# Two cross-attention layers on one core: another order in the prologue, one set of row scales for layer two, GpSimd's subtractions later in their window

## The reference

```python
q, k, v = x @ Wq, text @ Wk, text @ Wv
k_ip, v_ip = ip @ Wk_ip, ip @ Wv_ip
# layer one, each head
out = softmax(q k^T / sqrt(32)) v + softmax(q k_ip^T / sqrt(32)) v_ip
# layer two, each head; text_probs is over the full width of 640
text_probs = softmax(q @ k_text^T * scale)
sem = ((text_probs @ text) @ ip^T) * scale
ip_probs = softmax(q k_ip^T * scale + 0.5 * sem) * spatial_mask
out = softmax(q k^T * scale) v + ip_probs v_ip
x = out @ Wo + bo + x
```

## Time and profile before

| | us |
|---|---|
| median of three timed runs | 1839.28 |
| the profiled execution's own time | 1835.73 |
| its span, first to last instruction | 1833.9 |
| PE busy | 1763.1 (96%) |
| DVE busy | 1208.7 (66%) |
| ACT busy | 777.4 (42%) |
| POOL busy | 429.2 (23%) |

### The profile page before, as it was taken

How to read it: one execution, slowest core, us unless ns; L and a number is a source line. 1 busy time by engine, 2 the same in 40 slices (tenths; PEclk the granted TensorE clock), 3 DMA queues, 4 the chain that set the end, 5 groups by cost and what they waited for, 6 DMA issues and landing times. The chain is left out here.

```text
span 1833.9 us, 52042 instructions
## 1 busy us (share of the span) xinstructions
PE 1763.1 (96%) x22067; PEld 1420.8 (77%) x22067; DVE 1208.7 (66%) x2967; ACT 777.4 (42%) x1569; POOL 429.2 (23%) x520
## 2 busy tenths in 40 slices
PE   7988999999999999998999899999999999999998
PEld 4667888888888888885566688888888888888884
DVE  5775676767676767554654376767676767676673
ACT  3243554545545455453222243434444435344351
POOL 3031423334242433321100011211121212122120
PEclk9999999999999999999999999999999999999999
DMA  6742443434334344334146322414142324223221
GB/s 255 159 168 75 137 146 114 148 94 142 107 130 135 109 128 123 114 121 172 58 37 176 109 68 52 124 43 132 51 118 65 105 64 118 58 86 97 79 64 45
DMA packets 123583, 198.36 MB, mean 108 GB/s; under 512 B 41704, under 2 KB 110712, under 8 KB 116760
## 3 DMA queue, kind: packets, MB, share of 16 engines
q1 hardware_dynamic: 117880, 164.50, 31.4%
q10 hardware_dynamic: 5472, 30.54, 4.7%
HBM read 133.91 MB, written 60.88 MB: 106 GB/s over the span
## 5 line engine op out<-in xcount | busy, mean ns | idle before, releaser
L513 PE MATMUL proj<-w_hl,cbuf 128*128 128x128 f16 x9600 | 601.1, 219 | 0.7 <-issue 0.7
L513 PE MATMUL proj<-cbuf,w_hl 128*128 128x322 f16 (+1 forms) x3840 | 591.5, 300 | 2.7 <-issue 2.2
L513 PEld LDWEIGHTS proj<-w_hl,cbuf 128*128 128x128 f16 x9600 | 548.5, 98 | 2.8 <-issue 1.0
L513 PEld LDWEIGHTS proj<-cbuf,w_hl 128*128 128x128 f16 x3840 | 367.4, 97 | 166.5 <-issue 2.8
L1252 POOL TENSOR_TENSOR arena<-arena 128x400 f16<-128x400 f32 x240 | 235.9, 983 | 893.1 <-ACT arena L1011 893.1
L1010 ACT ACTIVATE arena<-st,rs 128x400 f16<-128x400 f32 x480 | 287.2, 598 | 285.3 <-DVE st L1634 167.7
L986 ACT ACTIVATE arena<-proj 128x323 f16<-128x323 f32 (+1 forms) x160 | 70.7, 442 | 516.5 <-PE proj L513 503.3
L1011 ACT ACTIVATE arena<-st,rs 128x400 f32<-128x400 f32 x480 | 285.8, 595 | 0.0
L1553 DVE TENSOR_TENSOR arena<-arena 128x400 f16<-128x400 f32 x240 | 144.9, 604 | 134.8 <-ACT arena L1011 131.7
L662 PE MATMUL pv<-arena 128*128 128x34 f16 (+3 forms) x3840 | 191.9, 189 | 6.9 <-POOL arena L1252 5.7
L662 PEld LDWEIGHTS pv<-arena 128*128 128x128 f16 x3840 | 173.5, 97 | 30.3 <-POOL arena L1252 9.4
(11 more groups left out here) (156 smaller groups left out, 1651.2 us busy)
## 6 DMA issues: line engine op xcount, KB each, us to landing
arena<-k_dram SPq DMA_DIRECT2D x240, 185.2 KB, 3.6
k_dram<-arena SPq DMA_DIRECT2D x160, 161.2 KB, 1.9
c_dram<-cbuf SPq DMA_DIRECT2D x16, 1290.0 KB, 6.4
raw<-ctx_dram SPq DMA_DIRECT2D x14, 1290.0 KB, 7.9
cbuf<-c_dram SPq DMA_DIRECT2D x12, 1290.0 KB
cbuf<-w_dram ACTq DMA_DIRECT2D x24, 640.0 KB, 7.3
arena<-q_dram SPq DMA_DIRECT2D x48, 125.0 KB, 2.6
cbuf<-c_dram ACTq DMA_DIRECT2D x2, 2580.0 KB
```

The costliest lines, as they stand in the source:

```text
L513: mm = nc.tensor.matmul(out, x[a](k), w[b](k), start=(k == 0 and m == 0), stop=(k == KT - 1 and m == 2))
```

## The change

- Start: a semaphore `warm` and 44 small matmuls on PE ahead of the q tiles. The text is loaded in two halves, one on SP's queue ahead of the constants, one on ACT's ahead of the weights (before: whole, on SP, behind the constants). DVE reduces the text first, then waits for the constants; half of the first weight's reductions, `weight_max` and `weight_scale` come behind the text's scale. PE turns the text's maxima ahead of q_tile(0, 1, 0). ACT splits the text ahead of the q tiles' evictions of the second half, and the first weight among them.
- SP at the first units: q and k are stored first and spread after; row 1's context (and its issue, which was ACT's) goes behind unit 1's k. ACT's waits on `kt_out` and `vt_out` go.
- PE: waits on `w_low` before the banks, each bank for itself (`vt`, `odd`); `odd_unit` waits for k's low of bank c only.
- Layer two's scales of all eight rows are made at once in `all_scales` (`rs1`, `back1`), `new_scale` and `row_scales` leave its windows.
- GpSimd in layer one's windows g = 1: `split_context` of slices 1 and 3 both behind the low of tile 5.
- PE in layer two's windows g = 3: three k's instead of two ahead of `max_scores(n, 0)`.

The diff, cut:

```diff
         def _(sp):
-            def place_q(r):
+            def store_q(r):
                 sp.wait_ge(q_lo_ok, r + 1)
                 if r >= 2:
                     sp.wait_ge(qp_in[r % 2], placed(r - 2, 48))
                     sp.wait_ge(s_full, NT * G * (r - 1))
                 sp.dma_start(qd[r % 2], qhl[:, :, 0:G * S]).then_inc(qw_out, 16)
+
+            def spread_q(r):
+
                 sp.wait_ge(qw_out, 16 * (r + 1))
                 for m, part in enumerate((0, 1, 0)):
                     sp.dma_start(qp[m * D:(m + 1) * D, r % 2, 0:G * Q4].rearrange("p (h q) -> p h q", h=HG),
                                  qd[r % 2][:, part].rearrange("(h d) q -> d h q", h=HG)).then_inc(qp_in[r % 2], 16)
-            def place_k(n):
+            def store_k(n):
                 b, g = n // G % B, n % G
                 for part, written in enumerate((k_high, k_low)):
                     sp.wait_ge(written, 2 * n + 2)
                     sp.dma_start(kd[b, g, :, part, IPO:KW], khl[:, part]).then_inc(kw_out[part], 16)
+
+            def spread_k(n):
+
+                b, g = n // G % B, n % G
                 need(sp, s_full, NT * (n - 1))
                 sp.wait_ge(kw_out[0], 16 * (n + 1))
                 for m in range(2):
...
             sp.dma_start(x_first, x_d[0]).then_inc(x_in[0], 16)
+            sp.dma_start(raw[:, 0:TH], text_d[:, 0:TH]).then_inc(text_in[0], 16)
             sp.dma_start(const[:], const_d).then_inc(const_in, 16)
             sp.dma_start(bias[:], bias_d).then_inc(const_in, 16)
             sp.dma_start(mask[:], mask_d).then_inc(const_in, 16)
-            sp.dma_start(raw[:], text_d).then_inc(text_in, 16)
             sp.dma_start(x_late, x_d[1]).then_inc(x_in[1], 16)
...
                 sp.dma_start(kp[IPO:P].rearrange("p b h t -> p (b h t)"), sel_d).then_inc(sel_in, 16)
                 if l:
                     place_kt(0)
-                place_q(l * B)
-                place_k(l * STEPS), place_k(l * STEPS + 1)
+                store_q(l * B), store_k(l * STEPS)
+                spread_q(l * B), spread_k(l * STEPS)
+                store_k(l * STEPS + 1), spread_k(l * STEPS + 1)
+                if l == 0:
+                    load_half(1, 0), load_half(1, 1)
                 sp.wait_ge(pads, l + 1)
                 place_vt(l * STEPS)
                 for c in range(2):
...
                 pe.wait_ge(w_low, 16 * (l + 1))
-                pe.wait_ge(k_low, 2 * l * STEPS + 4)
                 for c in range(2):
+                    pe.wait_ge(k_low, 2 * l * STEPS + 3 + c)
                     bank, full = bank_ready(pe, "odd", l, 0, c)
                     pairs(bank[:, 0:C // 2], texts(0, P), ip_weights(1, c * C // 2, (c + 1) * C // 2)
                           ).then_inc(full, 1)
...
+                begun = 3 if ahead and g == 3 else 2
                 if more2:
-                    k_part(k, 0, 0, 2)
+                    k_part(k, 0, 0, begun)
                 max_scores(n, 0)
                 if more2:
-                    k_part(k, 0, 2, 5)
+                    k_part(k, 0, begun, 5)
                 else:
...
+            pe.wait_ge(warm, 1)
+            for n in range(WARM):
+                nc.tensor.matmul(st[:, n % 2, 0:P], mxh[:, 0:P], mxh[:, 0:P], start=True, stop=True)
             for c in range(CT):
                 q_tile(0, 0, c)
-            q_tile(0, 1, 0)
             pe.wait_ge(const_in, 48)
             pe.wait_ge(ready, 2)
+            turn(ts, t_chain, 1, "text")
+            q_tile(0, 1, 0)
             weight_turn(0, 0)
-            turn(ts, t_chain, 1, "text")
             for c in range(1, CT):
                 q_tile(0, 1, c)
...
+            pe.wait_ge(w_low, 12)
             for c in range(2):
                 bank_done(pe, "vt", 0, TT - 1, c)
-            pe.wait_ge(w_low, 12)
-            for c in range(2):
                 k_part(0, c, 0, KT)
             weight_turn(0, 3)
             for c in range(2):
                 k_part(1, c, 0, KT)
             odd_unit(0)
-            for c in range(2):
-                bank_done(pe, "odd", 0, 0, c)
             for t in range(1, NT):
+                if t in (1, VA + 1):
+                    bank_done(pe, "odd", 0, 0, int(t > VA))
                 v_tile(0, t)
                 if t < NT - 1:
                     max_scores(0, t - 1)
...
+            pe.wait_ge(w_low, 28)
             for c in range(2):
                 bank_done(pe, "vt", 1, TT - 1, c)
-            pe.wait_ge(w_low, 28)
-            for c in range(2):
                 k_part(STEPS, c, 0, KT)
...
             act.dma_start(wq[:, 0], wq_d[0][:, 0]).then_inc(wq_first, 16)
             act.dma_start(wq[:, 1:], wq_d[0][:, 1:]).then_inc(wq_in, 16)
+            act.dma_start(raw[:, TH:], text_d[:, TH:]).then_inc(text_in[1], 16)
             load_weight(0, 0)
             q_tile(0, 0, 0), q_tile(0, 0, 1)
             load_weight(0, 1)
-            q_tile(0, 0, 2), q_tile(0, 0, 3), q_tile(0, 0, 4), q_tile(0, 1, 0)
-            split_weight(0, 0)
-            q_tile(0, 1, 1)
+            q_tile(0, 0, 2), q_tile(0, 0, 3), q_tile(0, 0, 4)
             act.wait_ge(t_chain, 5)
             for k in range(4):
                 split_text(k)
-            q_tile(0, 1, 2)
+            q_tile(0, 1, 0)
             for k in range(4, KT):
                 split_text(k)
-            q_tile(0, 1, 3)
+            q_tile(0, 1, 1)
+            split_weight(0, 0, (0, 1))
+            q_tile(0, 1, 2)
+            split_weight(0, 0, (2, 3))
+            q_tile(0, 1, 3), q_tile(0, 1, 4)
             load_weight(0, 2)
-            q_tile(0, 1, 4)
             kt_unit(0, 0), kt_unit(0, 1)
             split_weight(0, 1, (0, 1))
             kt_unit(0, 2)
...
             for c in range(2):
                 bank_done(act, "vt", 0, TT - 1, c)
             q_split(0)
-            act.wait_ge(kt_out[0], 96)
-            act.wait_ge(vt_out[0], 48)
             k_unit(0, 0), k_unit(0, 1)
-            for h in range(2):
-                split_done(act, 0)
-                act.dma_start(raw[:, h * CH:(h + 1) * CH], ctx_d[1][:, h * CH:(h + 1) * CH]).then_inc(ctx_in[h], 16)
             split_weight(0, 3)
             k_unit(1, 0), k_unit(1, 1)
             odd_unit(0)
...
-            act.wait_ge(kt_out[0], 192)
-            act.wait_ge(vt_out[0], 96)
             k_unit(STEPS, 0), k_unit(STEPS, 1)
...
                 if l == 0 and i < B - 1 and g == 1:
-                    chores = iter((lambda: (scale_context(r + 1, 3), split_context(r + 1, 1)),
-                                   lambda: split_context(r + 1, 3)))
+                    chores = iter((lambda: scale_context(r + 1, 3), lambda: None,
+                                   lambda: (split_context(r + 1, 1), split_context(r + 1, 3))))
                 if l == 0 and i < B - 1 and g == 2:
                     chores = iter((lambda: split_context(r + 1, 5), lambda: split_context(r + 1, 7)))
                 if l == 0 and i < B - 1 and g == 1:
...
-            nc.gpsimd.memset(mxh[:], 0.0)
+            nc.gpsimd.memset(mxh[:], 0.0).then_inc(warm, 1)
             nc.gpsimd.memset(pr[:], 0.0)
             nc.gpsimd.memset(odd_both[:], 0.0)
+            nc.gpsimd.memset(rs1[:], 0.0)
             nc.gpsimd.memset(rs[:], 0.0).then_inc(ready, 1)
...
+            def all_scales():
+
+                dve.wait_ge(units_ok, 4)
+                nc.vector.tensor_scalar(rs1[:, :, 0:4:2], wrow[:, 0:4:2].unsqueeze(1).to_broadcast([P, B, 2]), ts[:, 5:6],
+                                        None, ALU.mult)
+                for f in (1, 3):
+                    nc.vector.tensor_scalar(rs1[:, :, f], csb[:, :, 1], wrow[:, f:f + 1], None,
+                                            ALU.mult).then_inc(scale_steps, 1)
+                nc.vector.tensor_scalar(rs1[IPO:IPO + ODD, :, 6], csb[IPO:IPO + ODD, :, 0], wscale[IPO:IPO + ODD, 3:4],
+                                        VSC, ALU.mult, ALU.mult)
+                dve.wait_ge(scale_steps, 2 * B + 2)
+                nc.vector.tensor_copy(rs1[0:IPO, :, 4], rs1[0:IPO, :, 0])
+                nc.vector.tensor_copy(rs1[IPO:P, :, 4], rs1[IPO:P, :, 1])
+                nc.vector.reciprocal(rs1[:, :, 7], rs1[:, :, 1]).then_inc(scale_steps, 1)
+                dve.wait_ge(scale_steps, 2 * B + 3)
+                nc.vector.tensor_scalar(rs1[:, :, 5], rs1[:, :, 7], SEM * SC, None, ALU.mult).then_inc(row_scale, 1)
+                dve.wait_ge(row_scale, B + 1)
+                nc.vector.tensor_scalar(back1[:, :, 0], rs1[0:S, :, 2], 1.0 / VSC, None, ALU.mult).then_inc(back_ok, 1)
+                nc.vector.tensor_scalar(back1[:, :, 1], rs1[0:S, :, 3], 1.0 / VSC, mask[:, 1:2], ALU.mult,
+                                        ALU.mult).then_inc(back_ok, 1)
             def k_unit(n, c):
...
                         maxima(n, 0)
-                    if ahead and g == 0:
-                        new_scale(r + 1)
                     context_work(1)
                     maxima(n, 1)
```

(31 more changed lines are left out.)

35 lines of the change are left out of this document (19 added, 16 removed).

## The result

The changed kernel takes 1813.94 us, the median of four runs (1810.09 to 1815.84), where the kernel before, run beside it, takes 1840.09: a ratio of 0.9865, 95% interval 0.9845 to 0.9886. Two later comparisons gave 0.986 (0.9835 to 0.9885) and 0.9862 (0.9838 to 0.9886). The forecast was 1812, from 1802 to 1824.

A forecast was written before the change was run, and what follows sets the result against it. PE was busy 1763.1 of 1833.9 us, leaving about 71 us idle plus lower-clock matmuls to win. Six terms, from 1.6 to 6.6 us, sum to 26.9; off the timed median of 1839.28 that gave 1812, range 1802 to 1824.

The forecast's parts named there:

- The start: Prologue: shorter pauses and full clock let PE resume at 51.5 instead of 57.59; gain 6.1 us, bounds 3 and 8.5.
- the warm-up: 44 matmuls before the first tile could save 2.4 us, but waiting for wq until 12.5 swallows this.
- The case of wq on time: Upper bound at tile two: wq still lands near 10 us, worth +2.3 us.
- The first unit of layer one: Waits at layer one's first k and odd units shrink; gain 4.5 us, bounds 3 and 6.
- The step that said why the store lands earlier: Layer one: k's store issued before q's spreading, context behind all k; it lands near 131.5, odd_unit starts 3.9 us earlier.
- GpSimd's chores: Layer one, windows g = 1: moving two context subtractions behind tile 5's low gains 3.5 us, bounds 1 and 6.
- only 0.5 comes through: Of the 0.68 us wait per g = 1 window, DVE's reductions let 0.5 be gained, seven times.
- ends a few us later than now, in the time in which it idles: Layer one, g = 1: GpSimd's list runs later, within its idle time before the next window's first low.
- Layer two's scales and the third k: Layer two: windows g = 0 gain 7 x 0.94 = 6.6 us, windows g = 3 gain 7 x 0.23 = 1.6 us.
- Layer two's first unit: Storing k before q's spreading removes the 2.92 us pause and the slow row; gain 4.6 us, bounds 2.9 and 5.5.
- The bank wait gives nothing here: Layer two's first unit: waiting per bank gains nothing, as DVE's scales and low decide the next unit.
- The rival of a slower kernel: GpSimd's backlog stretches DVE's work by 4.3 us a window over seven windows, giving 1846; chance 0.03.

The follow-up runs named there:

- after again: The changed kernel run once more, unaltered, for a second trace; ratio 0.986 to the kernel before.
- the old windows: The changed kernel with its three edits inside the windows undone (GpSimd's subtractions, third k, DVE's scale instructions, these without their old waits); ratio 0.9877.
- the kernel with both waits old: The changed kernel with the odd unit waiting for both banks and q spread before k is stored, as before the change; ratio 0.9888.
- the kernel with the traded queue shares: The changed kernel with ACT's queue loading wq's rest then half the text, SP's queue the constants then the other half; ratio 0.9853.

## Why the prediction was right

*The start* was put at 6.1 with PE resuming at 51.5. The first trace has 52.62, after again 51.37. wq landed at 12.8 (12.5 said), the warm-up was swallowed, the pause ahead of the weight is 0.75 (1.0 said). The 1.1 us missing in the first trace are the clock's: 15.19 instead of 13.70 behind the 2.59 pause, which I had named as a bound. The case of wq on time, +2.3, is closed by the run that made it so and gained nothing. That PE no longer waits 3.66 is read from the traces; no run puts the weight ahead of the text again.

The row shows wq and the text moving at 51.4% and 50.9%, 0.66 and 0.65 MB in 3 us. The prediction weighed a rule of the Trainium skill (DMA: Bandwidth & Descriptors, Rules for kernel authors), that transfers spread over several issuing engines gain no bandwidth. The traces agree: both queues together moved 1.31 MB in these 3 us, and 1.30 MB before.

*The first unit of layer one* was put at 4.5: from PE's resuming to the shift turn it is 100.78 less 95.98, 4.8. The pause of 3.1, its end with DVE's lows and the slow row behind it are as written. The step that said why the store lands earlier named two causes; only the context is one.

The mean gain of this stage is 13.2 because the kernel before was dearer than its first trace: its pause of 5.96 was 7.15 the second time with 9.37 behind it for 8.03, and the row from 57.44 took 14.39 for 12.73. I took one trace's pause for the pause.

*GpSimd's chores* were mis-sized: 3.5 said, 7 x 0.32 = 2.2 measured. The step reads "only 0.5 comes through", and at its place it is right: from shift turn to second score row 12.71 before, 12.23 after. GpSimd's low at 352.38 now runs beside DVE's low of the context, 1.46 for 0.88, where it had run beside prob_low(4), 0.58 now for 1.06. The first of these costs nothing, since DVE had stood 0.65 idle behind it. But the shift turn itself now comes 1.81 us behind PE's last row ahead of it instead of 1.65, and that is the part that failed: GpSimd's list "ends a few us later than now, in the time in which it idles". That step overlooks a cast of `put_odd`, which stands ahead of that next window's lows and now falls on DVE's path. The cast, at 361.45, stood 1.67 us ahead of the shift turn in before's trace and stands 0.59 ahead now, beside DVE's first instruction of the shift, which takes 0.33 instead of 0.18. It is 0.32 to 0.39 in 20 of these 21 windows of the three traces of after and 0.18 in the one where the cast came earlier, in all seven of before, and in all seven with the old windows. That the stage gave 0.9 in the mean and not 2.2 is the slow row at 831 in the first trace and single windows 0.5 to 1.3 longer in the two others, where PE waited for a placement of k that came late; PE's timeline, after again:

```profile
636.69 0.39 PE L646 MATMUL rows<-arena 96*128 96x512 f16 x1 [1.28 <-DMA arena<-k_dram]
```

*Layer two's scales and the third k* are right: 18.23 to 17.29 and 24.47 to 24.26, 0.94 and 0.21 for 0.94 and 0.23. The stage gave 5.4 instead of 8.2 because of the slow rows near 1027 and 1765 (windows of 18.45 and 18.78 in two of three traces, and of 24.2 in all three, for 17.29 and 22.54). I had asked where an odd unit's clock might recover, and not whether a later pause would have the low one. It is not simply handed on, though: the kernel with both waits old has the slow odd unit again, and a slow row at 1030 too.

*Layer two's first unit*: 4.6 said. Pause and slow row are gone, and from k's first row (996.97 and 984.44) to the shift turn it is 46.8 less 42.5, 4.3. "The bank wait gives nothing here" is the step that failed. I reasoned from DVE's list that both banks are late together; the runs show that the first bank is enough for half of the odd unit, and that this wait alone leaves 0.76 of 3.17. The store's order, to which I gave the whole 2.92, leaves 1.10 when it stands alone. The remaining gain of the stage, up to 6.8, lies ahead of k's first row. Of it 0.7 is an edit that the sum left out in this layer: the wait there fell from 1.10 in both traces of before to 0.4, with w_low waited for first and each bank by itself; no run undoes that. The rest goes with the wait for v's store and the lower clock, which differ between traces.

The rival of a slower kernel rested on GpSimd's backlog stretching DVE by 4.3 us a window. Beside that backlog the reductions kept their 0.82; of what else was stretched, only the 0.15 at the shift's first instruction reached PE. Some slips of the prediction change nothing in this: the high ends of its terms add up to 35 and not 34, windows g = 1 at their neighbours' length would give 4.5 more and not 3, and the chance of slower is 0.03 in one place and 0.02 in another. Nor was DVE's row of 0.56 at 357.72 one without GpSimd, as it was read: a GpSimd instruction of 1.51 began 0.16 behind it. The row without one, in after, takes 0.58. So the sum, 26.9, met the medians' 26.2 by terms that were right to 0.3 us in five of six places, but for the clock at the start, and by luck: the errors of the stages, +2.6 and +2.2 against -2.6 and -2.8, cancel.

## What to carry to other kernels

Before pricing a pause from one trace, look whether its end hangs on a transfer or on the clock: here such pauses differ by 1 to 8 us between executions of the same code, while nearly all windows, which the engines pace, repeat to some 0.03 us. When two edits aim at one pause, undo each and both; either alone may carry nearly all. And taking a collision between VectorE and GpSimd away from one instruction is worth only what the instructions that inherit it can spare: one here had 0.65 us of idle time behind it, the other none.

## What the runs showed of the hardware

The lower clock level sits behind pauses of 0.6 to 8.5 us, but a given pause has it only in some executions: the one of 3.12 us ahead of layer one's odd unit in three of seven traces, the one of 2.22 near 1765 in nine of eleven traces of the changed kernel and its variants without a filler there, and the two of 1.5 ahead of layer two's first shift turn in ten of these eleven. In neither trace of before did it come behind the last two, though both have the same pauses. Two to seven such stretches stood in a trace of the changed kernel, 1.2 to 1.7 us each: a good part of what its runs differ by. What chooses among the pauses stays open.

Running beside GpSimd stretched some of VectorE's instructions and not others. Its subtraction of 128x400 took 1.06 us beside GpSimd and 0.58 alone, but 0.56 where it began 0.16 ahead of GpSimd's; its low of the context (128x645) took 1.46 instead of 0.88, a small instruction of 100x8 0.33 instead of 0.18, and a reduction from PSUM 0.81 or 0.82 either way.

A store of v beside the loads of four weight quarters and of 2.6 MB of context held ACT for 4.6, 8.3 and 13.5 us in three traces with the same code at this place; in the last PE paused 8.45 us, the median load of a weight quarter took 13.6 us from issue instead of 7.3, and that run was the slowest of its kernel, 1825.47. PE's timeline, from the kernel with the traded queue shares:

```profile
976.15 9.16 PE L540 MATMUL proj<-arena,t_hl 128*128 128x320 f16 x48 [8.45 <-DVE arena L1452]
```

What decides the length of that store was not tried.
